# Attention kernel: partial contexts stored and added late, a running minimum, three banks for turned quarters, and the rotation moved into the next super-tile

## What is computed

```python
x = _ln(src) * (1.0 + scale) + shift
q, k, v = ...                       # (x @ W + b), 16 heads of 32
scores = jnp.einsum('bhqd,bhkd->bhqk', q / math.sqrt(HEAD_DIM), k)
scores = scores + attention_bias    # [2, 16, 2048, 2048], f32, 537 MB
scores = jnp.where(src_mask, -jnp.inf, scores)
probs = jax.nn.softmax(scores, axis=-1)
ctx = jnp.einsum('bhqk,bhkd->bhqd', probs, v)
x = x + (ctx @ Wo + bo)
h = _ln(x) * g2 + beta2
ff = _gelu2(h @ W1 + b1) @ W2 + b2
# then every 4 columns of x + ff are rotated: two pairs, by theta and by phi
```

## Time and profile before

| | us |
|---|---|
| median of 3 runs | 3860.55 (3859.61 to 3860.59) |
| profiled execution | 3858.61 |
| its span, first to last instruction | 3857.0 |
| `phase_b`, first to last GpSimd pass | 519.4 to 2692.2 |
| `phase_c` begins | 2721.4 |

### The profile page before, as it was taken

How to read it: one execution, slowest core, us unless ns; L and a number is a source line. 1 busy time by engine, 2 the same in 40 slices (tenths; PEclk the granted TensorE clock), 3 DMA queues, 4 the chain that set the end, 5 groups by cost and what they waited for, 6 DMA issues and landing times. The chain is left out here.

```text
span 3857.0 us, 64984 instructions
## 1 busy us (share of the span) xinstructions
PE 3589.8 (93%) x18848; PEld 2074.9 (54%) x18848; DVE 2561.2 (66%) x4882; ACT 1899.6 (49%) x2483; POOL 2165.7 (56%) x595
## 2 busy tenths in 40 slices
PE   6778769999999999999999999999699999999997
PEld 2334336666666666666666666666344444444443
DVE  3444449999989999899999899999322323232232
ACT  1221227777777777777777777777211111111110
POOL 0000059999989999999999999999000000000000
PEclk8889879999999999999999999999799999999999
DMA  5556489999999999999999999997511101101000
GB/s 188 169 173 201 147 288 319 315 313 312 319 348 317 316 312 312 337 331 313 317 315 313 341 319 314 317 313 271 155 22 33 22 11 33 22 22 22 11 11 11
DMA packets 327444, 822.20 MB, mean 213 GB/s; under 512 B 165376, under 2 KB 181760, under 8 KB 250624
## 3 DMA queue, kind: packets, MB, share of 16 engines
q1 hardware_dynamic: 277376, 746.44, 57.6%
q10 hardware_dynamic: 45312, 58.74, 5.6%
q0 software_dynamic: 4736, 16.78, 1.2%
HBM read 737.95 MB, written 83.89 MB: 213 GB/s over the span
## 5 line engine op out<-in xcount | busy, mean ns | idle before, releaser
L450 POOL TENSOR_TENSOR ring<-ring,penb 128x2048 f32<-128x2048 f32 x512 | 2089.4, 4119 | 599.6 <-DMA penb<-pen_scratch 542.5
L555 ACT ACTIVATE ring<-ring,neg_max 128x2048 f32<-128x2048 f32 x512 | 1029.1, 2010 | 515.4 <-DVE neg_max L520 515.4
L618 PEld LDWEIGHTS b_T<-ident,ring 128*128 128x128 f32 x8192 | 886.7, 141 | 623.5 <-ACT probT L564 427.6
L618 PE MATMUL b_T<-ident,ring 128*128 128x128 f32 x8192 | 1158.7, 281 | 1.9 <-DVE probT L492 1.3
L492 DVE COPY probT<-b_T 128x512 f32<-128x512 f32 x1024 | 668.0, 684 | 70.5 <-PE b_T L618 70.5
L506 DVE CUSTOM_DVE_ANT_0 ring<-scores,ring,max_part 128x1024 f32<-128x1024 f32 x512 | 657.6, 1284 | 74.2
L506 DVE CUSTOM_DVE_ANT_0 ring<-scores,ring 128x1024 f32<-128x1024 f32 x512 | 622.2, 1215 | 43.6 <-PE scores L601 43.6
L601 PE MATMUL scores<-keys,queries 128*128 (+1 forms) x2048 | 606.5, 418 | 46.6 <-DMA queries<-q_parts 45.4
L781 POOL TENSOR_TENSOR y_out<-rot_a,rot_b 128x512 f32<-128x512 f32 x32 | 50.3, 1572 | 1020.8 <-DVE rot_b L890 1020.0
L564 ACT COPY probT<-b_T 128x512 f32<-128x512 f32 x1024 | 542.8, 580 | 30.2 <-PE b_T L618 24.0
L634 PE MATMUL bank_ctx<-probT,values 128*32 128x512 f32 x4096 | 546.8, 607 | 0.0
(11 more groups left out here) (91 smaller groups left out, 1926.1 us busy)
## 6 DMA issues: line engine op xcount, KB each, us to landing
ring<-in_fside_Bx16xSxS SPq DMA_DIRECT2D x512, 1024.0 KB, 5.8
keys<-k_parts SPq DMA_DIRECT2D x256, 256.0 KB, 6.8
values<-v_heads ACTq DMA_DIRECT2D x128, 256.0 KB, 6.0
queries<-q_parts SPq DMA_DIRECT2D x512, 64.0 KB, 6.8
pen_scratch<-pen SPq DMA_DIRECT2D x8, 2048.0 KB, 7.2
penb<-pen_scratch SPq DMA_DIRECT2D x32, 512.0 KB, 12.3
xin<-in_x ACTq DMA_DIRECT2D x8, 1024.0 KB, 5.2
mask_in<-in_mask_Bx1xSxS_bk ACTq DMA_DIRECT2D x8, 1024.0 KB, 7.3
```

What stands on the lines that cost most here:

```text
L450: nc.gpsimd.tensor_tensor(ring[:, j, :], ring[:, j, :], penb[:, j, :], ALU.add).then_inc(masked, 1)
L555: nc.scalar.activation(ring[:, k, :], ring[:, k, :], ACT.Exp, bias=neg_max[:, k:k + 1], accum_out=sums[:, k:k + 1]).then_inc(exp_done, 1)
L618: last = nc.tensor.transpose(bankT[n % 2][:, c * P:(c + 1) * P], ring[:, slot, at:at + P], ident[:])
```

## The change

In the attention stage:

- The partial contexts are stored as they are, 256 KB per unit instead of 64 KB. `close`, `bank_sum`, the reciprocal and the normalisation are gone from the stage.
- VectorE's second add gives the minimum of the negated values, `low`, which ScalarE uses as the bias with scale -1. The operation of L520 is gone. Sums and minima of all trips stay in SBUF (`sums_all`, `low_all`), for which ScalarE copies `low` once a trip, and VectorE's add of the next trip waits for that copy.
- The turned quarters use three banks. VectorE copies quarter 3 one step later, between its two adds, and quarter 2 after them.
- TensorE's waits for the exponent and for freed banks are put before a matmul that stands a little earlier in its list.

In the last stage:

- SyncE loads the partials of four heads (`parts`, 1 MB per block c, two buffers), GpSimd adds the four parts in two operations (1024 and 512 elements); in the first super-tile VectorE adds blocks 1 and 3.
- ScalarE widens the reciprocals of a block (`recip_wide`), TensorE turns them, VectorE multiplies them by the added context into `ctxT`. All of `front` is one block later.
- The rotation of super-tile u stands in `late(u, t)`, behind `hidden` of blocks 0 to 3 of super-tile u + 1; GpSimd's part with it. In super-tile 0 there is none.
- W1 and W2 are issued from ScalarE's list, after block 1 of the first super-tile has landed; Wo and the vectors after its blocks 0 and 1.

```diff
-        bankT = [ctx.enter_context(nc.psum_tensor(f"b_T{i}", [P, N], F32)) for i in range(2)]
+        bankT = [ctx.enter_context(nc.psum_tensor(f"b_T{i}", [P, N], F32)) for i in range(3)]
...
-        bank_sum = ctx.enter_context(nc.psum_tensor("bank_sum", [P, TOK], F32))
...
+            return bankT[(0, 1, 2, 0)[n] if t % 2 == 0 else (2, 1, 0, 2)[n]]
...
+                    nc.vector.tensor_tensor_reduce(out=at, in0=scores[c][:], in1=at, scale=-1.0,
+                                                   scalar=low_part[:, j:j + 1] if c else -MASKED,
+                                                   op0=ALU.add, op1=ALU.min,
+                                                   accum_out=low[:, j:j + 1] if c else low_part[:, j:j + 1]).then_inc(added, 1)
...
                 add(it, j, 0)
+                copy_quarter(it, j, 3, 3)
                 add(it, j, 1)
-                if live(i, NT):
-                    dve.wait_ge(added, i * CH + CH)
-                    nc.vector.tensor_scalar(neg_max[:, j:j + 1], max_part[:, j, CH - 1:CH], -2.0, 0.5, ALU.mult, ALU.mult).then_inc(max_ready, 1)
-                copy_quarter(it, j, 2)
...
-                copy_quarter(it, j, 3)
...
+                copy_quarter(it, j, 2, 2)
...
+                    k, trip = (j - 1) % R, it if j else it - 1
+                    act.wait_ge(added, i * CH)
+                    if j == 0:
...
+                        nc.scalar.copy(low_all[:, bass.ds(trip, 1), :].rearrange("p o n -> p (o n)"), low[:]).then_inc(low_kept, 1)
+                    nc.scalar.activation(ring[:, k, :], ring[:, k, :], ACT.Exp, bias=low[:, k:k + 1], scale=-1.0,
+                                         accum_out=column(sums_all, trip, k)).then_inc(exp_done, 1)
...
+                    act.wait_ge(ctx_stored, unit * 16 + 16)
+                    nc.scalar.copy(ctxp[:], bank_ctx[:]).then_inc(ctx_copied, 1)
...
+                                  ctxp[:]).then_inc(ctx_stored, 16)
...
+                    if n == CW // N - 1:
+                        free_before_turn(it, j, c)
...
+                    if c == 0:
+                        pe.wait_ge(exp_done, t + 1)
+                    else:
+                        need(pe, out_dve, t * 2 - 1)
...
+                if n == 2 and live(t, NT):
+                    need(pe, out_dve, t * 2)
+                for c in range(QR):
+                    if c == 2:
+                        if n == 0 and live(t, NT):
+                            need(pe, out_act, t * 2)
+                        if n == 1:
+                            copied_before_weigh(it, j)
+                        if n == 2 and live(t, NT):
+                            pe.wait_ge(out_act, t * 2 + 1)
...
                 turn(it, j, 1)
-                if j % QT == 2:
-                    close(it, j)
                 weigh(it, j)
...
                 for f in range(FB + 2):
                     ffn(u, f)
-                    if f < FB:
-                        front(u + 1, f)
+                    front(u + 1, f)
+                    late(u - 1, f)
...
+                    if isinstance(v, int) and c == 2:
+                        load_vectors()
+                    need(sp, ctxT_ready, v * DB + c - 1)
+                    for k in range(4):
+                        sp.dma_start(parts[DH * k:DH * (k + 1), c % 2, :, :],
...
+                nc.gpsimd.tensor_tensor(parts[:, c % 2, 0:2, :], parts[:, c % 2, 0:2, :], parts[:, c % 2, 2:4, :], ALU.add).then_inc(halved, 1)
+                pool.wait_ge(halved, added_by_pool(v, c))
+                nc.gpsimd.tensor_tensor(parts[:, c % 2, 0, :], parts[:, c % 2, 0, :], parts[:, c % 2, 1, :], ALU.add).then_inc(summed, 1)
...
+                add_parts(v, 0)
+                add_parts(v, 1)
+                finish(v - 2, 0)
+                finish(v - 2, 1)
+                add_parts(v, 2)
+                finish(v - 2, 2)
+                add_parts(v, 3)
+                finish(v - 2, 3)
...
+                if 1 <= f <= DB:
+                    c = f - 1
+                    act.wait_ge(recip_ready, v + 1)
+                    need(act, recip_turned, v * DB + c - 1)
+                    nc.scalar.copy(recip_wide[:, c % 2].rearrange("p t (h d) -> p t h d", d=DH),
+                                   recip[:, 4 * c:4 * c + 4, :].rearrange("p h (t o) -> p t h o", o=1).to_broadcast([P, QT, 4, DH])).then_inc(wide_ready, 1)
...
+            act.wait_ge(part_ld[1], 64)
+            for c in range(4):
+                act.dma_start(w1[:, :, c * D:(c + 1) * D], W1.rearrange("(c p) n -> p c n", p=P)[:, :, c * D:(c + 1) * D]).then_inc(w1_in, 16)
...
+                        nc.vector.tensor_tensor(parts[:, 1, 0:2, :], parts[:, 1, 0:2, :], parts[:, 1, 2:4, :], ALU.add).then_inc(first_summed, 1)
...
+                    dve.wait_ge(recip_turned, v * DB + c + 1)
+                    nc.vector.tensor_tensor(ctxT[:, c, :], fore[c % 2][:], parts[:, c % 2, 0, :], ALU.mult).then_inc(ctxT_ready, 1)
```

370 lines of the change are left out of this document (185 added, 185 removed).

## The result

| | median, us | runs | from, to |
|---|---|---|---|
| kernel before | 3860.3 | 4 | 3859.6, 3860.6 |
| kernel after | 3946.4 | 4 | 3923.2, 3974.1 |

A forecast was written before the change was run, and what follows sets the result against it. The prediction took VectorE's chain as the attention stage's bound before and GpSimd's passes after, TensorE in the last stage; -75.8 (attention), -47.0 (last stage) and +12.5 (its beginning) gave -110.3, so 3750 us, range 3723 to 3806.

The forecast's parts named there:

- -75.8 us: Attention stage: VectorE's last tile starts at 2626.6 us instead of 2702.4.
- GpSimd becomes the bound: Attention stage: VectorE's 3.76 and TensorE's 3.82 us a tile fall under GpSimd's unchanged 4.08 us pass.
- the changes of group: Attention stage: three later changes, each bringing 4.2 MB more mask, cost 3 us each, bounds 0 and 9.
- Rival B: Attention stage: transfers set the pace with 11.2 MB a trip; trips of 33.5 us, +54, 3804 us; chance 0.08.
- rival E: Attention stage: small TensorE waits in every tile lower its clock, 3.5 us a trip, +224, 3974 us; chance 0.05.
- A: Attention stage: hand-overs among VectorE, TensorE and ScalarE set the pace; trips of 33.2 us, +35, 3785 us; chance 0.17.
- C: Last stage: the load, addition, multiplication chain is late; TensorE waits 8 us in each of seven super-tiles, 3806 us; chance 0.08.
- D: Attention stage: the trip does not shorten, some wait replacing the closing; +76, 3826 us; chance 0.04.
- Rotation, -58.9: Last stage: moving the rotation behind four `hidden` removes 40.7 us of TensorE waits and 18.2 of slow `c_up` matmuls.
- stall, +11.9: Last stage: TensorE, turning block 0's reciprocals, waits 1.7 us for ScalarE's widened copy behind gate 1, seven times.
- GpSimd's additions: Last stage: adding partial contexts takes 3.1 to 6 us a block, costing 0, bound 10 in all.
- The beginning of the last stage: Stage start to first projection: 35 us instead of 22.4, +12.5, bounds +6 and +20.

The follow-up runs named there:

- the kernel with both edits: Kernel after, storing only 64 KB of the 256 KB partial contexts and requesting queries one tile earlier (output not the layer's): 3762.8 us, 0.9751 of before.
- the square: Kernel after with 256 or 64 KB stores, queries unchanged or a tile earlier: 3946.4 and 3822.8 us with 256 KB, 3788.6 and 3762.8 with 64 KB.
- the edit that removes it: Kernel after, ScalarE's widened copies one step earlier and its eight weight transfers behind the third copy: 3915.7 us, 1.0152 of before; super-tile period 127.17 us.
- queries in halves: Kernel after, queries loaded in two halves of 256 columns, six and seven tiles before use instead of four: 3881.8 us, 1.0069 of before.
- small stores: Kernel after, storing only 64 KB of the 256 KB partial contexts, last stage reading another tensor (output not the layer's): 3788.6 us, 0.9823 of before.
- bfloat16 and queries in halves: Kernel after with bfloat16 contexts, the last stage's order of ScalarE changed, and queries in two halves six and seven tiles ahead: 3774.2 us (3732 to 3813).

## Why the prediction was wrong, point by point

- **GpSimd's pass, VectorE's and TensorE's steps.** Right: passes of 4.11 to 4.12 us, an undisturbed step of 3.83, and trips of 32.6 in the kernel with both edits. The step "-75.8 us" holds for the computation: VectorE's last tile at 2620.0 there.
- **"GpSimd becomes the bound", so that "the stage's end follows from GpSimd alone": the step that failed.** It took every transfer as landing in time with 0.4 MB more a trip, and put the waits for them at nothing but the changes of group. The kernel after has 237.5 us of TensorE's waits for queries and 181.0 of GpSimd's for the bias (before: 45.4 and 55.8), and the term of -75.8 us came as +133.0. The rate was not far off: Rival B had full queues at 345 GB/s and a trip in 32.5 us by it (its 11.2 MB are 11.0, since the mean rate that it used takes in a change of group). At GpSimd's pace 338 are needed, 341 were moved for 293 us in one kernel with this volume, and 327 or 329 for long in others. What the proportion does not show is that nothing is left over: where the queues give less, or a load lands late, there is no slack to make it up. B's time, 3804, is near the 3822.8 of the change with earlier queries. It was given 0.08; transfers that take 32.5 us even by the hopeful reading, beside a trip of passes of 32.6, wanted far more.
- **The queries were no term at all.** The prediction went through waits, stores and weights, and never asked how long before their use the queries are requested, although 10 such waits stood in the profile's table of waits and it used their stretch (clock 0.96) for rival E. That lead is 11 us, against a median of 6.7 to landing, and the landing was about to grow. By the square, 98 of the 158 us that the volume costs go away with one tile more of lead.
- **Rival E** had the right end, slower, and nearly the time, 3974 against 3946. The mechanism was half right: TensorE's clock falls (0.94), but behind waits of some microseconds for queries, in every other half trip, and not by sub-microsecond waits in every tile. Its price of 3.5 us a trip stands against 1.6 us of slow step behind a wait, so the near time is luck.
- **Rivals A, C, D.** No hand-over sets the pace (the kernel with both edits has trips of 32.6), and C's and D's cases did not come up by themselves.
- **Rotation, -58.9, and stall, +11.9.** Right: 58.5 measured alone, 1.6 us seven times by the edit that removes it. GpSimd's additions take 2.42 and 1.33 us on average, 3.8 a block, in the lower part of 3.1 to 6, and no `c_up` waits for them.
- **The beginning of the last stage.** Mis-sized: +31.2 (first `c_up`) for +12.5 (35 - 22.4 is 12.6), the first projection 53.6 us after the stage's start for 35. The term at fault first is the price of ScalarE's eight issues: 0.79 us each, 6.3 in all, from 10 us after the stage's start. They begin at 11.4, once the first two blocks have landed, and take 16.2, so the first widened copy comes at 27.6 and not at 16. The row of 0.79 was GpSimd's; ScalarE's own, beside the other loads, were 1.2 and 2.8 each. Block 2 takes 12.6 us from request to addition for 9, and block 3 lands only after VectorE has used block 1 and waits its turn beside 8.4 MB of weights.
- **Of the two places of the Trainium skill.** "DMA: Bandwidth & Descriptors", Specifications, gives about 358 GB/s a core. No kernel with full queues moved that for long: 329 to 337 GB/s over 1500 us, 341 over 293. By the page a trip's 11.0 MB would take 30.7 us (an estimate) and hide behind GpSimd with 2 us to spare; by the measured rates they take 32.3 to 33.7 and have next to nothing to spare. The measurement decides. The exclusion of VectorE and GpSimd ("SBUF — State Buffer", SBUF: two separate sides) shows in the last stage, as the prediction had it: a rotation operation of 0.34 us takes 2.44 beside an addition of GpSimd. It is behind no wait of TensorE there. Timeline of all engines of the kernel after:

```profile
3088.61 2.47 POOL L796 TENSOR_TENSOR parts<-parts 128x1024 f32<-128x1024 f32 x1 [3.84 <-DMA parts<-ctx_scratch]
3088.78 2.44 DVE L961 TENSOR_SCALAR rot_b<-y,sines 128x128 f32<-128x128 f32 x1
```

## What to carry to other kernels

Before a change adds bytes to a stage whose transfers are busy over 0.9, divide a trip's bytes, the new ones included, by the pace of the engine that is to bound it. If the rate that comes out (338 GB/s here) is no clear distance below what full stretches of the kernel move (327 to 341 here), there is no slack, and every late load costs time. Then list each load with the time from its request to its use, beside the median time to landing: here a load with 11 us of cover against a median of 6.7 turned a busier queue into stalls of TensorE, and a stall can cost its clock too. Moving a sum to a later stage moves its operands through memory; here four times the bytes of contexts cost more than the matmuls that they replaced. With half of those bytes, one request a tile earlier and a shorter beginning of the last stage, the same idea is 3% faster than before; of these 119 us the late rotation and the earlier queries on the old attention stage have 71 by themselves (3788.8).

## What the runs showed of the hardware

- Over 1500 us with a share of 0.99 to 1.01 seven kernels moved 329 to 337 GB/s. One of them, at a share of 1.02 both times, moved 341 in one stretch of 293 us and 327 in another of 300 with the same transfers. Why the same share moves different amounts is open.
- On the kernel before, 3.7% more bytes (0.39 on 10.6 MB a trip) took the bias from 5.8 to 8.3 us to landing, the queries from 6.7 to 7.0, and TensorE's waits for queries from 10 to 32. In the change the medians are 10.4 and 8.3, and 14.9 for the bias with the queries in halves.
- After a wait of 2.5 us the next score matmuls ran at the lower clock level (2.02 us instead of 1.2 to 1.3), and the whole step took 5.45 us for 3.83.
- Issuing four weight transfers held ScalarE for 11.3 us in one place and 26.4 in another, with copies behind it, at shares of 1.11 and 1.06. SyncE was held 8.8 us by the same four, and the first projection came 12 us earlier.
- VectorE's operation of 0.34 us took 2.44 beside a GpSimd addition of 2.47.
- With the volume of the change, executions of one kernel differed by 0.9 to 1.6%, with small stores by 0.9% and with bfloat16 and queries in halves by 2.2%; the kernel before and its late-rotation forms stayed within 0.3%.
